# Folding the output weights into the value weights of a six-layer local attention kernel

## The reference, cut to what matters

```python
for i in range(6):                                      # x: [b, 256, 128]
    x = attn_layer(shift_tokens(x), Wqkv[i], ..., Wo[i]) + x
    x = ffn_layer(shift_tokens(x), ...) + x

def attn_layer(x, Wqkv, qs, ksc, Wo):                   # 16 heads of 64
    q, k, v = split(x @ Wqkv)                           # 3 x 1024 columns
    q, k = rotary(l2norm(q) * qs), rotary(l2norm(k) * ksc)
    out = local_attention(q, k, v)                      # windows of 32 queries, 64 keys
    return out.transpose(0, 2, 1, 3).reshape(b, n, 1024) @ Wo   # Wo: [1024, 128]
```

## Time and profile before

| | |
|---|---|
| median of 3 runs | 4073.27 us (4065.49, 4073.51, 4073.27) |
| span of the profiled execution | 4069.5 us |
| PE / DVE / ACT / POOL busy | 91% / 76% / 72% / 58% |
| normalisation, to the first DMA of the next block | 43.5 us |
| delta mixer | to about 686 us |
| transformer | from about 686 us to the end |
| one body of the transformer in the middle | 34.33 us |

### The profile page before, as it was taken

The page is one execution under the profiler, slowest core; times in us unless marked ns, Lnnn a source line. Parts: engine busy times, 40 slices in busy tenths (PEclk is TensorE's granted clock), DMA queues, the critical chain, the costliest instruction groups (busy, mean ns, idle before and its releaser), DMA issues.

```text
span 4069.5 us, 138077 instructions
## 1 busy us (share of the span) xinstructions
PE 3712.5 (91%) x57362; PEld 3044.3 (75%) x57362; DVE 3102.3 (76%) x5808; ACT 2923.2 (72%) x5487; POOL 2362.8 (58%) x2271
## 2 busy tenths in 40 slices
PE   4757654899999999999999999999999999999998
PEld 3746542688888888888888888888888888888886
DVE  4386675778888888888888888887888888888883
ACT  2423223688888888888888888888888888888885
POOL 1111111666666666666666666666666666666662
PEclk9777665999999999999999999999999999999999
DMA  2000000433333333334333334333333333343332
GB/s 62 23 28 2 11 12 9 109 101 91 88 89 97 108 86 91 91 91 119 91 91 91 87 98 108 88 90 91 102 108 91 91 88 88 99 107 93 99 95 53
DMA packets 149452, 331.77 MB, mean 82 GB/s; under 512 B 17632, under 2 KB 27616, under 8 KB 147168
## 3 DMA queue, kind: packets, MB, share of 16 engines
q1 hardware_dynamic: 148832, 322.93, 30.2%
HBM read 218.01 MB, written 104.86 MB: 79 GB/s over the span
## 4 chain that ended last, share of the span: by engine, by line
PE 62%; POOL 9%; ACT 7%; issue 3%; DVE 2%; POOLq 0%; ACTq 0%; DVEq 0%
PE bank L1697 17%; PE bank L1814 8%; PE bank L1756 7%; PE bank L1787 7%; PE bank L1734 7%; PE bank L1855 7%; PE bank L1802 4%; ACT L1418 3%; POOL qk L1158 3%; PE bank L1771 2%; POOL qk L1168 2%; POOL pr L1177 2%; ACT sq L1240 2%; PE bank L1839 2%; ACT pT L1289 1%
## 5 line engine op out<-in xcount | busy, mean ns | idle before, releaser
L1158 POOL TENSOR_TENSOR qk<-rot_a,rot_b 128x512 f32<-128x512 f32 x768 | 984.9, 1282 | 684.0 <-PE bank L1734 644.1
L1168 POOL TENSOR_TENSOR qk<-qk,rn 128x512 f32<-128x512 f32 x768 | 797.7, 1050 | 71.2 <-DVE rn L1576 71.2
L1497 DVE TENSOR_TENSOR rot_a<-bank,rot 128x512 f32<-128x512 f32 x768 | 530.9, 691 | 303.7 <-PE bank L1697 273.1
L1240 ACT ACTIVATE sq<-bank 128x512 f32<-128x512 f32 x768 | 458.6, 597 | 264.2 <-DVE rot_b L1504 261.9
L1697 PE MATMUL bank<-w_hi,xs_hi 128*128 128x512 f32 x1152 | 573.8, 498 | 59.9 <-ACT pT L1289 20.9
L1512 DVE TENSOR_REDUCE ss<-sq 128x8 f32<-128x512 f32 x768 | 513.7, 669 | 96.4 <-ACT sq L1240 96.3
L1177 POOL TENSOR_TENSOR pr<-pr,prec 128x512 f32<-128x512 f32 x384 | 399.4, 1040 | 290.3 <-DVE prec L1541 290.3
L1504 DVE TENSOR_TENSOR rot_b<-bank,rot 128x512 f32<-128x512 f32 x768 | 522.7, 681 | 0.0
L1734 PE MATMUL bank<-ident,qk 128*128 128x128 f32 x3072 | 463.4, 273 | 6.9 <-ACT qT L1251 3.9
L1697 PE MATMUL bank<-w_lo,xs_hi 128*128 128x512 f32 x1152 | 458.9, 398 | 0.0
L1697 PE MATMUL bank<-w_hi,xs_lo 128*128 128x512 f32 x1152 | 457.9, 397 | 0.0
(11 more groups left out here) (238 smaller groups left out, 7161.5 us busy)
## 6 DMA issues: line engine op xcount, KB each, us to landing
vw<-value_scratch SPq DMA_DIRECT2D x576, 256.0 KB, 5.0
value_scratch<-v SPq DMA_DIRECT2D x192, 512.0 KB, 2.6
vw<-value_scratch SPq DMA_DIRECT2D x192, 192.0 KB, 4.0
stage<-in_wqkv SPq DMA_DIRECT2D x6, 1536.0 KB, 9.0
stage<-in_wb_all SPq DMA_DIRECT2D x6, 1088.0 KB, 9.7
stage<-in_band SPq DMA_DIRECT2D x6, 512.0 KB, 5.1
d_xt<-in_x SPq DMA_DIRECT2D x4, 512.0 KB, 3.8
base_scratch<-d_res SPq DMA_DIRECT2D x4, 512.0 KB, 3.3
```

The lines of the kernel that those rows point to most:

```text
L1158: nc.gpsimd.tensor_tensor(qk[:, c, :], rot_a[:, c % 2, :], rot_b[:, c % 2, :], ALU.add)\
L1168: nc.gpsimd.tensor_tensor(y, y, rn[:, x.q, 8 * c:8 * c + 8].unsqueeze(2).to_broadcast([P, 8, DH]), ALU.mult).then_inc(S["scaled"], 1)
L1240: nc.scalar.activation(sq[:, :], proj_bank(x, c)[:, :], ACT.Square).then_inc(S["squared"], 1)
L1497: nc.vector.tensor_tensor(rot_a[:, c % 2, :].rearrange("p (h d) -> p h d", h=8), proj_bank(x, c)[:, :].rearrange("p (h d) -> p h d", h=8), ...
```

## The change

The product `Wv_h @ Wo_h` (128x64 by 64x128) is made once for each layer and head in `normalise_input`: 96 small products on PE, copied by ACT and written by SP to a scratch `vo_d` in device memory. `value` then projects onto these 16 x 128 = 2048 columns instead of 1024, in 8 pieces instead of 4, in two banks in turn (`ps_p`, `ps_g`). `weigh` has as many matmuls as before, but all heads add up in the same 128 columns of `ps_o`. What comes out is the layer's output by tokens; `mixed_out` copies 128 columns for each half and `turn_mixed` turns them with two transposes into `ps_c`. `heads_taken`, `turn_heads`, `heads_out` and `join_heads` are gone. The window scratch and `vw` hold twice the bytes, and the scratch is written by a new step `keep` in four parts. `stage` now holds all 16 sequences of the mixer's result at the end (before: 13, and 3 later). The orders of PE, ACT, DVE and POOL in `body` are new.

```diff
@@ normalise_input @@
         def _(sp):
             sp.dma_start(xt[:, :, :], x_d.rearrange("b (u p) d -> p (b u) d", p=P)).then_inc(s_in, 16)
+            for l in range(DEPTH):
+                sp.dma_start(wv[:, l, :], wv_d[l, :, :]).then_inc(s_weights[2 * l // DEPTH], 16)
+                sp.dma_start(wo[:, l, :], wo_d[l, :, :]).then_inc(s_weights[2 * l // DEPTH], 16)
+            for i in range(2 * DEPTH):
+                sp.wait_ge(s_fold, 2 * i + 2)
+                sp.dma_start(vo_d[i // 2, :, i % 2 * 2 * CK:(i % 2 + 1) * 2 * CK],
+                             fold[:, i % FOLD_SLOTS, :, :].rearrange("p e n -> p (e n)")).then_inc(s_folds[i % FOLD_SLOTS], 16)
...
+            def fold_out(i):
+                act.wait_ge(s_product, i + 1)
+                if i >= FOLD_SLOTS:
+                    act.wait_ge(s_folds[i % FOLD_SLOTS], 16 * (i // FOLD_SLOTS))
+                for e in range(2):
+                    nc.scalar.activation(fold[:, i % FOLD_SLOTS, e, :],
+                                         ps_fold[2 * (i % 2) + e][:, :, :].rearrange("p c n -> p (c n)"), ACT.Copy).then_inc(s_fold, 1)
+            for i in range(FOLD_FIRST):
+                fold_out(i)
             for g in range(NT // 4):
...
+            for i in range(FOLD_FIRST, 2 * DEPTH):
+                fold_out(i)
...
+                for c in range(NPAIR // 2):
+                    for e in range(2):
+                        head, cols = slice(e * DH, (e + 1) * DH), slice((r * 4 + c) * P, (r * 4 + c + 1) * P)
+                        mm = nc.tensor.matmul(ps_fold[2 * (i % 2) + e][:, c, :], wv[head, l, cols], wo[head, l, cols],
+                                              start=True, stop=True)
@@ local_transformer, SP @@
+            def keep(x, half, r):
+                need(sp, S["v_out"], x.u * 8 + 4 * half + 2 * r + 2)
+                need(sp, S["valued"], x.u * 4 - 5)
+                sp.dma_start(v_d[x.u % 2, half * P:(half + 1) * P, r * INNER:(r + 1) * INNER], v[:, r, :])\
+                    .then_inc(S["v_kept"], 16)
+                sp.wait_ge(S["v_kept"], 16 * (4 * x.u + 2 * half + r + 1))
...
-                        sp.dma_start(vw[rows, slot(x, half), w:4, r, :],
-                                     kept[first:last, r * CK:(r + 1) * CK].rearrange("(w p) n -> p w n", p=WIN))\
+                        sp.dma_start(vw[rows, slot(x, half), w:4, :, :].rearrange("p w c n -> p w (c n)"),
+                                     v_d[x.u % 2, first:last, r * INNER:(r + 1) * INNER].rearrange("(w p) n -> p w n", p=WIN))\
...
             def body(b):
                 new, turn, att, out, ffn = b.items
+                keep(turn, 0, 0)
+                keep(turn, 0, 1)
                 window(turn, 0)
+                keep(turn, 1, 0)
+                keep(turn, 1, 1)
                 window(turn, 1)
@@ ACT @@
+                if n % 2 == 0:
+                    need(act, S["v_kept"], 16 * (4 * x.u + n // 2 - 1))
+                nc.scalar.activation(v[:, n // 2 % 2, n % 2 * CK:(n % 2 + 1) * CK], value_bank(n)[:, :], ACT.Copy)\
...
+            def mixed_out(x, half):
+                need(act, S["valued"], x.u * 4 + (2 * half + 2))
+                need(act, S["mixed_turned"], x.u)
+                nc.scalar.activation(o_tok[:, half, :], ps_o[:, 0:P], ACT.Copy).then_inc(S["o_out"], 1)
@@ PE @@
-                        first = (4 * e + c) * DH
-                        mm = nc.tensor.matmul(ps_o[w * WIN:(w + 1) * WIN, c * P:(c + 1) * P].rearrange("p (r d) -> p r d", r=2),
-                                              pT[:, k % 2, c, w * WIN:(w + 1) * WIN],
-                                              vw[:, slot(x, half), w, :, first:first + DH],
-                                              start=True, stop=True, skip_group_check=True)
+                        mm = nc.tensor.matmul(ps_o[w * WIN:(w + 1) * WIN, 0:P], pT[:, k % 2, c, w * WIN:(w + 1) * WIN],
+                                              vw[:, slot(x, half), w, 4 * e + c, :],
+                                              start=e == 0 and c == 0, stop=e == 1 and c == 3, skip_group_check=True)
...
+            def turn_mixed(x):
+                need(pe, S["o_out"], x.u * 2 + 2)
+                need(pe, S["layer_out"], x.u)
+                for half in range(2):
+                    mm = nc.tensor.transpose(ps_c[:, half * P:(half + 1) * P], o_tok[:, half, :], ident[:, :])
+                mm.then_inc(S["mixed_turned"], 1)
```

More of the change, by code:

```diff
@@ L1370, in body @@
                 high_half(b, new)
+                exp(out, 3)
+                square_centred(ffn)
+                mask_scores(att, 1)
+                square(turn, 7)
+                probs_out(out, 2)
+                mixed_out(out, 0)
+                if b.switch == -2 and not b.first:
+                    convert(b.layer, 3, "projected", turn.u * 8 + 8)
+                roots(turn, ffn)
+                mask_scores(att, 2)
+                value_out(turn, 0)
+                value_out(turn, 1)
@@ new lines, in body @@
+                square(new, 0)
+                if b.first and b.edge == -2:
+                    zero_values(0)
+                turned_out(att, 7)
+                exp(att, 0)
+                affine(ffn)
+                turned_out(turn, 0)
+                probs_out(out, 3)
+                square(new, 1)
+                if b.first and b.edge == -2:
+                    zero_values(1)
+                gelu(ffn)
+                turned_out(turn, 1)
+                value_out(turn, 2)
+                if ffn.there:
+                    nc.scalar.preload_act_table_set(EXP_LN_TABLE)
@@ L1371, in body @@
+                square(new, 2)
+                if b.first and b.edge == -2:
+                    zero_values(2)
+                exp(att, 1)
+                turned_out(turn, 2)
+                probs_out(att, 0)
+                mask_scores(att, 3)
+                mixed_out(out, 1)
+                square(new, 3)
+                value_out(turn, 3)
+                turned_out(turn, 3)
                 if b.switch == 1:
                     need(act, S["loaded_b"], b.layer * 16 + 16)
-                    need(act, S["wo_done"], out.u)
@@ L1400, in body @@
-                value_out(turn, att, 0)
-                gelu(ffn)
-                turned_out(turn, 0)
-                probs_out(out, 3)
-                square(new, 2)
-                if b.first and b.edge == -2:
-                    for i in (4, 5):
-                        zero_values(i)
-                turned_out(turn, 1)
-                heads_taken(out, 3)
-                mask_scores(att, 3)
-                turned_out(turn, 2)
-                value_out(turn, att, 1)
-                square(new, 3)
@@ L1902, in body @@
[L1902 to L1903 removed]
+                value(b, turn, 3)
+                turn_qk(turn, 3)
                 ffn_out(ffn)
[L1905 removed]
                 query_key(b, new, 4)
[L1907 to L1909 removed]
+                value(b, turn, 4)
+                value(b, turn, 5)
                 turn_qk(turn, 4)
[L1911 removed]
+                turn_mixed(out)
@@ L1920, in body @@
+                mean(out)
                 turn_qk(turn, 6)
                 query_key(b, new, 7)
-                value(b, turn, 3)
-                score(turn, 0)
-                if b.switch == 1:
-                    need(pe, S["conv_act"], b.layer * 2 + 2)
-                    need(pe, S["conv_dve"], b.layer + 1)
-                mean(out)
+                turn_probs(att, 2, turn, 3)
+                weigh(att, 0)
                 weigh(att, 1)
-                turn_probs(att, 2, turn, 3)
```

413 lines of the change are left out of this document (179 added, 234 removed).

## The result

The changed kernel takes 4226.81 us (median of 4 runs, 4220.1 to 4240.35) beside 4073.14 us for the kernel before on the same chip: a ratio of 1.0388, 95% interval 1.0368 to 1.0407. The forecast was 3930 us, with a range that ended at 4030. The time is outside it, and on the other side of no change.

A forecast was written before the change was run, and what follows sets the result against it. PE was taken as the bound. 4069.5 - 92 bodies x 1.75 (161) + 17 start + 5 layer changes - 4 end = 3926.5, given as 3930 us; forecast 3885 to 3985, 8-in-10 range 3875 to 4030.

The forecast's parts named there:

- That is below 32.6, so it hides.: SP's loop of doubled windows and scratch writes: 28.7 us, below the 32.6 us body, so no cost.
- PE's work: In each body, PE sheds 5.25 us and gains 3.12 and 0.22: net 1.9 us less.
- the cost of the four projection pieces: On PE in each body, four added projections at 0.78 us each: 3.12 us more.
- The wait for `sq`: On PE before query/key piece 3, a new wait for ACT's square: 0.4 to 0.5 us a body.
- Layer changes: Weight loads queue between windows and the next write: 1 us on each of 5 changes, +5 us.
- The start: Making and storing the weight products delays the next block's first DMA by 16 us, its loads by 1: +17 us.
- The end: In the last unit, running alone, `join_heads` and one group of transposes leave the path: about -4 us.
- the DMA engines' share: Sign of being right: DMA engines 60 to 70% busy in a body.
- the cadence: Sign of being right: POOL's `low_half` comes every 32.3 to 32.9 us.
- the window above 10 us: Sign of being wrong: a window read takes more than 10 us.
- the slower one, 4198: Rival: SP's loop bounds the body, deciding from 182 GB/s down; at 160 GB/s the kernel takes 4198 us; chance 0.09.
- The new orders wait more: Rival: further waits in the new engine orders cost 0.7 to 1.5 us a body, 4030 us; chance 0.15.

The follow-up runs named there:

- fine: The changed kernel with one 128 KB DMA for each 32-token window, partitions 0 to 63 and 64 to 127 in turn: 3877.4 us, ratio 0.9526.
- paced: The changed kernel, but SyncE issues the third and fourth 512 KB DMA of each window only when the first two have landed: 4294.35 us, ratio 1.0541.
- small: The changed kernel with 128 KB DMAs, one for each 32-token window, in the changed kernel's own sequence: 3922.67 us, ratio 0.9643.
- halfjunk: The changed kernel reading half of each window's columns, the columns left out copied to an unused place in device memory: 3900.29 us.
- traffic: The kernel before, with window copies inside device memory added for its first 60 units, in eight DMAs of 2 KB rows a body: 4071.34 us.

## Why the prediction was wrong, by its own steps

**The step that failed** is the one on the DMAs, "That is below 32.6, so it hides." It set the doubled windows against one reader only, SyncE's own loop. For that it held: ACT's copies to `v` wait for a DMA 16 times in 2400 us, some 66 bodies, and SyncE itself waits 1135.9 us of them for ACT to have copied `v`. But the same 16 DMA engines also bring PE its instructions. A window of 2.1 MB issued in 1.75 us and moved at 194 to 213 GB/s is a queue of about 10 us, twice the 4.76 of the earlier trace rows, and the q8 packet starts as it ends. PE used up a block in 2400 / 271 = 8.9 us, so a fetch that is held for 5 us comes in time and one that is held for 10 can't. (That last step is an estimate from the rows, not a measurement; what the traces show is that no q8 packet of the changed kernel starts more than 288 instructions ahead of the place where PE would stop, little over one block.) The kernel before had no row that showed a wait; it had q8's share, 0.8%, and the sum has no term for it.

**What it cost.** 181.1 us over 66.2 bodies is 2.7 us a body. For the clock: PE's busy time in the same 2400 us is 2190.49 / 33585 = 65.2 ns a matmul, beside 2344.91 / 37374 = 62.7 in fine; by 507 matmuls a body, 1.3 us. Together 4.0. Against that, PE's other waits are 28.4 us in the 2400, 0.4 a body, beside 55.1 or 0.75 in fine, so 0.3 comes off: 3.7. Measured are 36.23 - 32.69 = 3.54 us a body. Over the 96 units that is 340 us, and the two profiled spans differ by 4225.9 - 3884.6 = 341.

**PE's work: right in mechanism, undersized.** Forecast was a body of 32.6; undisturbed it is 32.04 to 32.09. PE is busy for 31.7 us in it, not 34.05: 2.35 us less, not 1.9. The term that was oversized is the cost of the four projection pieces: the prediction took 0.78 us for one behind another, from two starts, but the chain has three in 2.09 us at full clock (2083.46 above), 0.70 each. With 4 x 0.70 = 2.8, and the 5.36 of the chain that the prediction cut to 5.25, it is 5.36 - 2.80 - 0.22 = 2.34. `weigh` costs 1.01 us for 32 records as before, so accumulating cost nothing here.

**The wait for `sq`: right.** 30.5 us in 2400, 0.42 us a body in fine, beside 0.45; 0.35 in the row at 2076.53.

**Layer changes: undersized.** Forecast +5 in all. In fine bodies are 32.69 in the mean from 1100 us on, 32.09 undisturbed: 81 x 0.6 = 49 us of longer bodies, beside 82 x 0.15 = 12 before. Some 40 us more, of which the 13.7 us under ACT `v` are the part that these views name.

**The start: oversized, then worth nothing.** The mixer's first DMA goes out at 54.93 us, 11.5 later than in the earlier trace rows, not 17:

```profile
54.93 0.33 SPq L309 DMA_DIRECT2D d_wproj<-in_wproj  x1
...
735.49 0.72 POOL L1205 TENSOR_TENSOR xs_lo<-stateT,xs_hi 64x256 fp32r<-64x256 f32 x1
```

By the third `xs_lo` it is made up: 735.49, where the kernel before has 736.52.

**The end: undersized.** From the last `xs_lo` to the end it is 4069.5 - 3938.7 = 130.8 us before and 3884.6 - 3772.5 = 112.1 in fine, 19 less; the prediction put 4 on the end. Not followed further.

**The signs.** Of the signs of being right, the DMA engines' share came true (0.69), the `sq` wait too, the cadence (36.23) and the mixer's start (54.93, not 60) not. Of the signs of being wrong, the window above 10 us came true: 2065.92 to 2078.47 from first issue to last landing. The forecast's rates, 212 and 220 GB/s, came out as 194 in that window. The 2 us plus bytes / 436 GB/s, which the prediction quotes from the Trainium skill as general, is given there for DMAs that GpSimd issues; here SyncE issues them. No term of the sum used it.

**The rivals.** The time is near that of the slower one, 4198, but that is luck: its mechanism, windows slower than 182 GB/s in SyncE's loop, is not what happened. It does exist: the paced runs show it. "The new orders wait more" has at most a small part: with `weigh(att, 0)` back at its old place (apart) the stops are 122.3 us and not 181.1, and the time is 38 us shorter.

**What stays open.** Shown is that the stops are late instruction fetches, that they come with the window DMAs, and that the late packets start as a window ends. At 512 KB a DMA, issuing two at a time instead of four removes nearly all of them. In fine and small the DMAs are shorter and also issued over a longer time, and no run has many short DMAs queued at once, so the two are not told apart there. Why copies inside device memory do not do the same (halfjunk, traffic: as many bytes, hardly any stops) is only argued: they move faster, 0.17 of a 32.6 us body or 5.5 us for 1.97 MB, some 350 GB/s, so the queue is shorter. And whether the fetch waits in a DMA engine's own queue, or on the way into memory, no view tells.

## What to carry to other kernels

Price a larger DMA not only against the one who waits for its data, but by how long it keeps the DMA engines full at one stretch: PE's instructions come through the same engines, and a PE-bound kernel of many small matmuls needs a new block every few us (8.9 here). If PE stops with "issue" in the midst of a group, count the records from stop to stop; a constant count, or a multiple of it, points to instruction fetches. What cured it here was to queue less at once, in shorter DMAs that are issued over time. A pause with a wait for landing cured the stops too, but it lengthened the loop of the engine that issues, and the kernel got slower.

## What the runs showed that I had not expected

- A q8 packet of 16 KB stands for 248 records of PE and PEld: 271 packets for 33585 + 33584 in the changed kernel, 301 for 37374 + 37373 in fine. With the semaphore instructions it is 256. Of the 88 distances between stops in the changed kernel 54 are two packets long, 26 are four, one is 20, and 7 are odd.
- A stop of 1.96 us was followed by a granted clock of 0.56 and then 0.50 for over 3 us; one of 2.13 us was not. In paced, where PE waits for `v` and `sq` and hardly stops, the clock was low for 229 us of 2400, in the changed kernel for 208.
- The same bytes take 0.60 of the DMA engines when DMAs of 128 KB go to partitions 0 to 63 and 64 to 127 by turns, and 0.73 when they fill 32 partitions after 32.
- A source access pattern whose outermost dimension is 2 brought 73 GB/s.
